# Roots of two groups in one GpSimd operation, and their statistics in pairs, in the first routing of a mixture-of-experts block

## The reference, cut to what matters

```python
x = x + _L0_attn_a_ref(_layernorm(x), ...)             # the last product and sum are done inside the routing
x = x + _L0_ffn_ref(_layernorm(x), ...)

def _L0_ffn_ref(x, ...):                               # 8 experts, two for each token
    residual = x
    mu = jnp.mean(x, axis=-1, keepdims=True)
    var = jnp.mean((x - mu) ** 2, axis=-1, keepdims=True)
    xn = (x - mu) * jax.lax.rsqrt(var + EPS) * ln_gamma + ln_beta
    abel_out = _gelu(xn @ abel_w + abel_b)
    logits = xn @ moe_gate_w + moe_gate_b
    topw, topi = jax.lax.top_k(logits, 2)
    topw = jax.nn.softmax(topw, axis=-1)
    ...                                                # experts, rotation, gate
```

## Time and profile before

| | |
|---|---|
| median of three runs | 1333.04 us (1325.3, 1333.04, 1333.91) |
| the profiled execution's own time | 1330.22 us |
| its span | 1328.6 us |
| TensorE (PE) busy | 1174.7 us, 88% |
| VectorE (DVE) busy | 864.5 us, 65% |
| ScalarE (ACT) busy | 494.2 us, 37% |
| GpSimd (POOL) busy | 412.5 us, 31% |
| mean granted TensorE clock | 0.933 of full speed |
| roots on GpSimd in the tile `work` (L723) | 24 operations, 39.6 us |

### The profile page before, as it was taken

The page is one execution under the profiler, slowest core; times in us unless marked ns, Lnnn a source line. Parts: engine busy times, 40 slices in busy tenths (PEclk is TensorE's granted clock), DMA queues, the critical chain, the costliest instruction groups (busy, mean ns, idle before and its releaser), DMA issues.

```text
span 1328.6 us, 25931 instructions
## 1 busy us (share of the span) xinstructions
PE 1174.7 (88%) x7208; PEld 1015.1 (76%) x7209; DVE 864.5 (65%) x2777; ACT 494.2 (37%) x961; POOL 412.5 (31%) x490
## 2 busy tenths in 40 slices
PE   7988978787999999965999989999756999999988
PEld 6746657665888889954789878888645888998977
DVE  6768767746666666676866677776444666666666
ACT  1104623334444444432333433343333344444445
POOL 3003116752444444420000000115553344444420
PEclk8998968878999999987999999999868999999989
DMA  9401313435444533351011110001225633443358
GB/s 296 136 8 64 128 64 146 168 130 189 136 136 139 163 95 87 94 191 48 1 49 49 49 48 1 1 9 57 96 80 197 237 120 119 128 154 108 103 186 281
DMA packets 72688, 149.15 MB, mean 112 GB/s; under 512 B 10950, under 2 KB 36754, under 8 KB 72602
## 3 DMA queue, kind: packets, MB, share of 16 engines
q1 hardware_dynamic: 52234, 93.40, 20.3%
q0 software_dynamic: 19584, 53.92, 13.4%
q10 hardware_dynamic: 784, 0.79, 0.2%
HBM read 82.63 MB, written 65.44 MB: 111 GB/s over the span
## 4 chain that ended last, share of the span: by engine, by line
PE 59%; issue 7%; DVE 6%; another core or an unknown queue 5%; ACT 4%; DMA 2%; POOL 1%; POOLq 1%; SPq 1%; DVEq 0%; ACTq 0%
PE bank L2430 17%; PE bank L1967 9%; PE bank L1968 8%; PE bank L1969 8%; PE bank L1827 5%; PE bank L1996 4%; PE bank L1979 2%; PE bank L2488 2%; PE bank L2049 2%; DMA xh<-slots_in 1%; POOL xh L1553 1%; DVE work L2209 1%; DVE xs L2196 1%; PE bank L2441 1%
## 5 line engine op out<-in xcount | busy, mean ns | idle before, releaser
L1967 PE MATMUL bank<-ew,rows 128*128 x852 | 298.8, 351 | 5.4 <-DVE rows L1420 3.7
L1968 PE MATMUL bank<-low_in,rows 128*128 x852 | 274.1, 322 | 0.0
L1969 PE MATMUL bank<-ew,rows 128*128 x852 | 272.6, 320 | 0.0
L1565 POOL DMA_INDIRECT results<-xh x142 | 141.9, 999 | 291.5 <-DVE xh L1448 271.6
L1967 PEld LDWEIGHTS bank<-ew,rows 128*128 128x128 f32 x852 | 161.6, 190 | 16.6 <-issue 8.9
L1969 PEld LDWEIGHTS bank<-ew,rows 128*128 128x128 f32 x852 | 161.4, 189 | 11.3
L1968 PEld LDWEIGHTS bank<-low_in,rows 128*128 128x128 f32 x852 | 162.3, 190 | 6.0
L1794 ACT ACTIVATE xh<-bank 128x512 f32<-128x512 f32 x142 | 84.9, 598 | 219.2 <-PE bank L1969 219.2
L1457 DVE TENSOR_TENSOR rows<-bank,rows 128x512 fp32r<-128x512 f32 x142 | 98.2, 692 | 94.0 <-ACT rows L201 86.5
L723 POOL TENSOR_TENSOR work<-work,mhalf 128x8 f32<-128x8 f32 x24 | 39.6, 1649 | 314.8 <-DVE work L716 302.1
L1827 PE MATMUL bank<-abw,work 128*128 128x8 f32 (+1 forms) x512 | 109.3, 361 | 15.9 <-ACT ab L1757 9.3
(11 more groups left out here) (371 smaller groups left out, 2043.5 us busy)
## 6 DMA issues: line engine op xcount, KB each, us to landing
xh<-slots_in POOLq DMA_DIRECT2D x138, 129.0 KB
low_in<-low SPq DMA_DIRECT2D x32, 512.0 KB
ew<-results SPq DMA_DIRECT2D x7, 1032.0 KB, 8.4
xh<-results SPq DMA_DIRECT2D x6, 1032.0 KB, 5.2
dense<-ab SPq DMA_DIRECT2D x12, 512.0 KB
xs<-in_L_attn_a_x_dram SPq DMA_DIRECT2D x4, 1024.0 KB, 7.9
ew<-in_L_ffn_ew_dram SPq DMA_DIRECT2D x2, 2048.0 KB, 13.3
ew<-in_L_ffn_ew_dram SPq DMA_DIRECT2D x4, 1024.0 KB, 14.7
```

Of the source, the lines that this page charges most:

```text
L1565: pool.indirect_dma_start(out=yg, out_offset=bass.IndirectOffsetOnAxis(ap=back[j % RING], axis=0), in_=yr[j % RING], in_offset=None).then_ ...
L1967: pe.matmul(o, hi, f32r(high(c)), start=(c == 0), stop=False)
L1968: pe.matmul(o, hi, f32r(low(c)), start=False, stop=False)
L1969: last = pe.matmul(o, lo, f32r(high(c)), start=False, stop=(stop and c == chunks[-1]))
```

## The change

Only the first routing changes (`r == 0`).

- **GpSimd.** The roots of group 3 stay as they are, in the middle of the scatters of group 0. In the middle of group 1 one operation of 16 numbers per partition now makes the roots of groups 4 and 5, and in the middle of group 3 one makes those of groups 6 and 7. In the middle of groups 2 and 4 there is nothing any more.
- **VectorE.** The statistics of group 5 are made right behind those of group 4 (step 1), and those of group 7 right behind those of group 6 (step 3). Steps 2 and 4 have none.
- **TensorE.** attend(5) moves from behind route(2) to ahead of it, attend(7) from behind route(4) to ahead of it.
- The wait of `normalise` counts operations of GpSimd, so its numbers change with them.

```diff
@@ normalise
-                v.wait_ge(nrm.root_ok, g + 1)
+                v.wait_ge(nrm.root_ok, {5: 5, 6: 6, 7: 6}.get(g, g + 1) if r == 0 else g + 1)
@@ vector
-                    if r == 0 and g + 3 < NG:
-                        statistics(v, g + 3)
+                    for h in ({0: (3,), 1: (4, 5), 3: (6, 7)}.get(g, ()) if r == 0 else ()):
+                        statistics(v, h)
@@ gpsimd
-                        if r == 0 and t == h * GT + HALF and h + 3 < NG:
-                            nrm.roots(pool, h + 3)
+                        if r == 0 and t == h * GT + HALF and h in (0, 1, 3):
+                            nrm.roots(pool, {0: 3, 1: 4, 3: 6}[h], 1 if h == 0 else 2)
@@ tensor
+                    if r == 0 and p in (2, 4):
+                        attend(pe, p + 3)
                     if p < NG and ORDER[p] >= EARLY_GROUPS:
                         route(ORDER[p])
-                    if r == 0 and p + 3 < NG:
-                        attend(pe, p + 3)
+                    if r == 0 and p in (0, 1, 3):
+                        attend(pe, {0: 3, 1: 4, 3: 6}[p])
```

## The result

The changed kernel took 1343.54 us, the median of four runs (1341.34 to 1345.17). The kernel before took 1333.47 us, the median of four (1325.3 to 1333.92; three of them are the runs that were on record before). The medians differ by 10.1 us. The ratio on record is 1.0105, with a 95% interval of 1.0076 to 1.0134. The forecast was 1330, and the range ended at 1341. The profiled execution took 1343.8 us with a span of 1342.2 us, which is 13.6 us more than the profiled execution of before.

What follows compares the result with a forecast made beforehand. It took the first routing as bound by a ring of hand-overs, no engine full. The terms summed to -0.5 us, 1329.7 from the profiled 1330.22; forecast 1330, between that and the median 1333.04 less 0.5, range 1320 to 1341.

Steps and rivals of the forecast that it cites:

- GpSimd's scatters: GpSimd, first routing: pairs push scatters back, missing roots return 1.85 us each; group 5's end 1.5 us later, covered by idleness.
- Step 4: VectorE at choose(3): ready 1.5 us earlier, but logits still come at 238.25 unless the unnamed stall changes; 0 gained.
- unnamed stall: Before choose(3): ScalarE copies group 3's logits only at 238.02, after 6.88 us of idleness the profile cannot name; taken as unchanged.
- Step 1: VectorE: choose(2) starts at 225.9 instead of 222.20, behind statistics(5); attend(5) is ready in time at 221.9.
- slower rival: TensorE between rank(2) and group 3's logits: stall moves along, clock falls, choose(3) 3.4 us late; 1336.9 us, chance 0.2.
- Step 2: TensorE: route(2), now behind attend(5), runs from 221.9 to 223.8 and costs nothing, with 2 us of cover.
- Step 3: GpSimd's first pair starts at 225.9 and ends at 229.1; VectorE's 1.18 us wait before normalise(4) is gone, just.
- faster rival: The stalls go: choose(3) at 233.4, 4.8 us earlier, 1328.3 us; 1321.9 if the piece at 274.50 goes too; chance 0.2.
- Step 5: VectorE from choose(3) to choose(4): 13.2 us instead of 9.57, one statistics more; choose(4) at 251.5 instead of 247.82.
- Step 6: GpSimd's second pair runs from 251.5 to 254.7; VectorE's 0.53 us wait before normalise(6) is gone, with no margin.
- Step 7: VectorE from choose(4) to choose(5): 7.56 us instead of 11.73; choose(5) at 259.1 instead of 259.55.
- late roots rival: Statistics(5) or (7) delayed by TensorE hold back GpSimd's pair; attend(7) 2 us late gives 1331.7, inside the forecast's 0.6.

Runs made afterwards that it cites:

- e2_attend_ahead_only: The kernel before with only TensorE's order changed: attend(5) and attend(7) ahead of route(2) and route(4), statistics and roots single; ratio 1.0003 to the kernel before.
- e12_more_pauses_again: The kernel before plus idle power operations on GpSimd in the middle of groups 5, 6 and 7, on a chip with late signals; 1322.93 us, ratio 0.9944.
- e14_before_drains: The kernel before, with GpSimd waiting in the middle of groups 5, 6 and 7 until all scatters so far have landed; 1321.66 us, ratio 0.9972.
- e7_before_more_pauses: The kernel before plus idle power operations on GpSimd in the middle of groups 5, 6 and 7, on the chip without late signals; 1292.46 us, ratio 1.0009.

## Why the prediction was wrong, step by step

**The step that failed** is where the roots that disappear from groups 2 and 4 were costed, under "GpSimd's scatters", as 1.85 us of GpSimd's time given back each. As work they are just that. As the only pause in a row of scatters they also let signals of TensorE through, and that was put at nothing. Without them group 3's count, done at 239.34, was read at 248.18, and this one wait of 7.61 us is three quarters of the delay at choose(4). Step 4 has the same fault in its "unless the unnamed stall changes": it took the stalls for a given, with no cause that the change could touch. Putting the single roots back (`e3_single_roots`) brings the time back to 1.0019, whose interval reaches down to 0.9999.

The clue was in the trace of before. The unnamed stall ended at 238.02, between a start of roots at 237.11 and its end at 238.78. The prediction read ScalarE and GpSimd one after the other and never laid them beside each other.

By its other steps:

- **The roots.** 16 numbers took 2.93 us (227.74 and 257.98), predicted 3.2, bounds 1.65 and 3.30. The upper end was the right one. By an estimate from the Trainium skill's rule of about 2.6 cycles per element (GPSIMD Engine Reference, section 3.1) it would have been 1.67; the trace doesn't agree with it for this operation, since eight more numbers cost 2.93 - 1.65 = 1.28 us.
- **Step 1, choose(2).** Predicted at 225.9, measured at 227.56. attend(5) took 3.78 us instead of 2.00: TensorE had stood idle for 2.10 us, and the granted clock, 1.00 up to 218 us, was 0.52 from 220 to 222, the low level of 1.2 GHz. VectorE's addition had to wait for it, 1.38 us. That the clock might fall one piece earlier stood in the slower rival; it did, but `e2_attend_ahead_only` shows that it costs nothing in the end.
- **Step 2, route(2).** Predicted free, by 2 us of cover. It lasted 3.42 us at the low clock, until 227.09, ScalarE's copy of the logits ended at 227.48, and choose(2) began at 227.56 with no wait. Right, but with 0.1 us of cover left.
- **Step 3.** The wait of 1.18 us for the roots is gone, as predicted. The pair began at 227.74 instead of 225.9, for the reason of step 1, and ended at 230.67, and normalise(4) followed at 230.85.
- **Step 4.** choose(3) came at 235.39 and not at 238.25. The stall there became 1.94 us. The faster rival had the direction right, and forecast 233.4. The rival gave no reason why the stall should go.
- **Step 5.** Failed, as above: choose(4) at 257.80, not 251.5.
- **Step 6.** The wait of 0.53 us is gone, as predicted.
- **Step 7.** From choose(4) to choose(5) it was 8.59 us, predicted 7.56. Nearly all of the difference is a gap of 0.97 us before choose(5).
- **The late roots rival** was real in a small way: attend(7), late by the 7.61 us, held GpSimd's second pair for 3.35 us (257.98). GpSimd's scatters of group 3 could start only at 249.87, after 4.02 us of waiting for addresses, where the prediction expected no gap.

The last sentence of the prediction named the danger: stalls that fall elsewhere without any term being wrong. It was given no price and no chance of its own. The slower rival had the right sign and 1336.9 us, but neither half of its mechanism: choose(3) came at 235.39 and not at 241.7, and the clock is ruled out by `e2_attend_ahead_only`.

**Better than both.** `e12_more_pauses_again` (ratio 0.9944) and `e14_before_drains` (0.9972) are both faster than the kernel before, on chips where signals are late; on the chip where they are not, the program of the first is level with it (`e7_before_more_pauses`, 1.0009).

**What stays open.** Why scatters hold TensorE's signals, whether by their issue or by their transfers, and why one chip of those used doesn't show it. What lets a signal through in the middle of a row stays open too, as four of the changed kernel's nine did. How long a row of scatters must be isn't regular either: the logits of group 3 came through at 235.16 after 4 us of it, and in the kernel before those that ended at 230.07 didn't, 3 us after its row began. That the signals are held, and not TensorE itself, is read from the ends of its matmuls, which are modelled in the profile; the waits of two engines that end together within 0.14 us, 2.2 us behind the last scatter, speak for it. How the loss divides among the waits wasn't separated further either, nor whether single roots (1.0019) bring back more than two operations of 1.5 us in the same places (1.0026 twice); their intervals overlap.

## What to carry to other kernels

Where an engine issues indirect DMAs in a long row, ask of each operation between them what else gets through while it runs, before you merge it with another. And a stall that the profile can't name is not a constant: lay the moments at which such stalls end beside what every other engine started or stopped then, and price the change for its doing away with that. On a chip of this kind, look whether a pause in the row is worth more than it costs, and measure on more than one chip.

## What the runs showed of the hardware

- While GpSimd issued indirect DMAs without a pause (0.96 us each and 0.30 us between them), signals of TensorE reached ScalarE and VectorE late, by waits of up to 12.80 us. More than half of these waits ended during or right behind another operation of GpSimd, in a gap, or 2.0 to 2.7 us after the last scatter of a row (7 of 11 in the kernel before, 5 of 9 in the changed one); the others ended in the middle of a row. Pauses of 1.5 us and more made the kernels faster (0.9944 and 0.9972 of the kernel before), memsets of 0.1 us did not (1.0075 beside 1.0057).
- It depends on the chip. The kernel before took 1291.54 us on one, and 1325.26 to 1333.47 in the other sets. The traces differ in those waits, which stand in both routings in those of the kernel before and of `e12_more_pauses_again`, and the same program, up to its first scatter of the routing, ran at the same pace on both kinds (277.47 and 277.63 us to the reading of group 7's count).
- Raising to a power on GpSimd took 1.51 us for 7 numbers per partition, 1.65 for 8 and 2.93 for 16: about 0.16 us per number and 0.37 us fixed, worked out from the last two.
- With TensorE's new order alone (`e2_attend_ahead_only`) an idle time of 2.11 us stands ahead of attend(5), the granted clock of that 20 us stretch was 0.75 instead of 1.00, and the whole kernel's time didn't change (1.0003).
